# First attention: projections of 16 pieces placed in the attention's plan, row scores of the first heads beside them, low parts of the rotation on GpSimd

## What is computed

```python
x = x + 0.5 * _L0_ffn_ref(_layernorm(x), ...)
x = x + _L0_attn_ref(_layernorm(x), Wq, Wk, Wv, Wo)      # the changed part
x = x + 0.5 * _L0_ffn_ref(_layernorm(x), ...)

# _L0_attn_ref: B, S, H = 2, 1024, 256; 16 heads of 16
q, k, v = proj(Wq), proj(Wk), proj(Wv)
q, k = _apply_rope(q, cos, sin), _apply_rope(k, cos, sin)
scores = einsum('bhqd,bhkd->bhqk', q, k) / sqrt(hd) + causal
probs  = softmax(scores)
out    = einsum('bhqk,bhkd->bhqd', probs, v) @ Wo.T
```

## Time and profile before

| | us |
|---|---|
| median of 3 timed runs | 2742.62 (2741.81 to 2753.49) |
| profiled execution, whole | 2735.0 |
| its span | 2733.2 |
| PE busy in the span | 2529.4 (93%) |
| DVE busy | 1847.8 (68%) |
| ACT busy | 1396.2 (51%) |
| POOL busy | 369.8 (14%) |
| second tail of phase 0 ends on PE | 145.1 |
| first projection piece starts | 160.8 |
| last projection piece and values end | 226.3 |
| first T step starts | 275.55 |

### The profile page before, as it was taken

The page is one execution under the profiler, slowest core; times in us unless marked ns, Lnnn a source line. Parts: engine busy times, 40 slices in busy tenths (PEclk is TensorE's granted clock), DMA queues, the critical chain, the costliest instruction groups (busy, mean ns, idle before and its releaser), DMA issues. The chain is left out here.

```text
span 2733.2 us, 49842 instructions
## 1 busy us (share of the span) xinstructions
PE 2529.4 (93%) x16744; PEld 2111.5 (77%) x16744; DVE 1847.8 (68%) x4018; ACT 1396.2 (51%) x2464; POOL 369.8 (14%) x279
## 2 busy tenths in 40 slices
PE   3975898869899999998999999999999999999999
PEld 3963445358788888887877877878877788888888
DVE  4566767456567777776766766767767677777773
ACT  3430555645455555554655655555555555555553
POOL 1000000010121222221110010001100222122220
PEclk9996989879999999999999999999999999999999
DMA  4026133000000000000000000000000000000000
GB/s 157 0 78 146 25 48 48 2 32 4 27 31 22 10 31 31 0 20 20 1 20 1 19 19 0 19 19 0 19 0 32 32 32 1 32 31 0 31 0 31
DMA packets 18930, 73.28 MB, mean 27 GB/s; under 512 B 3328, under 2 KB 8192, under 8 KB 15616
## 3 DMA queue, kind: packets, MB, share of 16 engines
q1 hardware_dynamic: 18816, 71.78, 9.2%
HBM read 61.02 MB, written 10.49 MB: 26 GB/s over the span
## 5 line engine op out<-in xcount | busy, mean ns | idle before, releaser
L349 PEld LDWEIGHTS ps<-w,hid 128*128 128x128 f32 x5376 | 698.9, 190 | 56.5 <-DVE rb L425 14.6
L349 PE MATMUL ps<-w,hid 128*128 128x256 f32 x5376 | 719.5, 284 | 2.5 <-DVE rb L425 1.5
L318 PE MATMUL ps<-xT,w 128*128 (+1 forms) x2688 | 703.9, 398 | 0.1
L502 DVE TENSOR_TENSOR hid<-gel,hid 128x512 fp32r<-128x512 f32 x448 | 403.4, 911 | 360.8 <-ACT hid L392 352.4
L386 ACT ACTIVATE gel<-ps,b 128x512 f32<-128x512 f32 x448 | 306.9, 686 | 557.3 <-issue 543.6
L318 PEld LDWEIGHTS ps<-xT,w 128*128 128x128 f32 x2688 | 479.6, 190 | 79.5 <-issue 0.3
L392 ACT ACTIVATE hid<-gel 128x512 fp32r<-128x512 f32 x448 | 272.9, 622 | 0.0
L864 PE MATMUL ps<-pT,v_sb 128*128 128x512 f32 (+3 forms) x1152 | 261.6, 358 | 1.9 <-DVE pT L982 1.9
L838 PE MATMUL ps<-k_sb,q_sb 128*128 128x512 f32 (+3 forms) x1152 | 252.7, 353 | 3.0 <-DVE q_sb L999 3.0
L971 DVE TENSOR_REDUCE negmax<-ps 128x1 f32<-128x128 f32 (+7 forms) x256 | 192.3, 752 | 76.8 <-PE ps L841 75.5
L1431 DVE TENSOR_REDUCE nmx<-ps 128x1 f32<-128x512 f32 (+3 forms) x384 | 196.2, 553 | 70.1 <-PE ps L1302 53.5
(11 more groups left out here) (118 smaller groups left out, 2884.1 us busy)
## 6 DMA issues: line engine op xcount, KB each, us to landing
wraw<-in_wffn SPq DMA_DIRECT2D x12, 2048.0 KB, 7.7
wraw<-in_w_a SPq DMA_DIRECT2D x8, 1280.0 KB, 5.4
qk_dram<-rope_hl SPq DMA_DIRECT2D x16, 512.0 KB, 3.0
xT<-qk_dram SPq DMA_DIRECT2D x60, 128.0 KB, 8.3
qk_own<-qk_dram SPq DMA_DIRECT2D x36, 128.0 KB, 6.4
xb<-in_wffn SPq DMA_DIRECT2D x2, 2048.0 KB, 13.0
x<-in_x SPq DMA_DIRECT2D x4, 512.0 KB, 5.5
rot<-in_rot SPq DMA_DIRECT2D x1, 2048.0 KB, 18.7
```

Source lines behind the costliest of these rows:

```text
L318: last = nc.tensor.matmul(ps[:, HPS + j % 4, :], w[par][:, wp, 0, k * HIDDEN + j * PART:k * HIDDEN + (j + 1) * PART], xT[:, xp, k, bass.ds ...
L349: last = nc.tensor.matmul(y_ps[:, t, :], hid[:, hp, j % 4, t * PART:(t + 1) * PART], w[par][:, wp, 1, j * DIM:(j + 1) * DIM], start=j == 0 ...
L502: nc.vector.tensor_tensor(hid[:, 1, j % 4, :], gel[:, j % 4, :], hid[:, 0, j % 4, :].bitcast(f32), ALU.subtract).then_inc(low_done, 1)
```

## The change

1. The 16 projection pieces become items P of the plan. Their order is such that the first four (chunks 0 and 1, half 0, query and key) carry everything that groups 0 and 1 of heads need, the next four the other half of chunks 0 and 1, and the last eight chunks 2 and 3.
2. The tail of phase 0 (items S, L, G: the last second matmuls and take, the pieces of the norm, the transposes with the affine and the low input) is placed among the first four pieces, which need only chunks 0 and 1.
3. The splits of the attention's weights move into the first chunk of phase 0 (steps 4 to 7 of its eight).
4. Values are made two tiles at a time (12 matmuls of 256 columns, one copy of 512 elements), after pieces 4 to 11, in the PSUM bank of A.
5. From piece 6 on, three pairs U of row scores follow each piece: 30 of the 32 pairs of the lead stand among the pieces.
6. DVE keeps multiplies and sums; POOL makes the low parts of all 16 pieces, and its memsets stand among them (ones of the first buffers and of `v_f` after low part 1, of the second after low part 9, of the third after low part 15).
7. SP issues `load_heads(0)` after the store of piece 4, `load_heads(1)` after that of piece 9, and `load_heads(2)` after the feed-forward weights as before.
8. Buffers are laid out anew (`qk_own` becomes `q_own` and `k_own`, the third slot of `pT0` becomes `pT0_last`), so that the weights lie where phase 0 does not read.

```diff
+        PIECES = [(chunk, qk, half) for chunks, halves in (((0, 1), (0,)), ((0, 1), (1,)), ((2, 3), (0, 1)))
+                  for chunk in chunks for half in halves for qk in range(2)]
+        V_FROM, U_FROM, U_EACH = 4, 6, 3
...
+        def pool_rope_a0(pool):
+            def low_part(n):
+                pool.wait_ge(rope_high, n + 1)
+                nc.gpsimd.tensor_tensor(rope_hl[:, 1, n % 2, :], rope[:, 2, n % 2, :],
+                                        rope_hl[:, 0, n % 2, :].bitcast(f32), ALU.subtract).then_inc(rope_low, 1)
...
+            for n in range(N_PIECES):
+                low_part(n)
+                if n == 1:
+                    ones(QK[0])
+                    nc.gpsimd.memset(v_f[:], 1.0).then_inc(v_ones, 1)
+                if n == 2:
+                    nc.gpsimd.memset(nmx[:], 0.0).then_inc(v_ones, 1)
+                if n == 9:
+                    pool.wait_ge(proj_ready, 8)
+                    pool.wait_ge(v_ready, QT // 2)
+                    ones(QK[1])
+            pool.wait_ge(proj_ready, N_PIECES)
+            pool.wait_ge(v_ready, TILES // 2)
+            ones(QK[2])
...
+            for n in range(N_PIECES):
+                token, seq, qk, half, slot = rope_piece(n)
                 sp.wait_ge(rope_low, n + 1)
                 sp.dma_start(qk_dram[qk, half * PART:(half + 1) * PART, :, bass.ds(token, CHUNK)],
                              rope_hl[:, :, slot, :].bitcast(f32)).then_inc(rope_stored[slot], 16)
-                if n == N_PIECES // 2:
+                if n == 4:
...
                     sp.wait_ge(k_ones, 1)
                     load_heads(0)
+                if n == 9:
+                    sp.wait_ge(k_ones, 2)
+                    load_heads(1)
             sp.wait_ge(a_low, 4)
             load(1, 0, xb_raw)
             sp.wait_ge(k_ones, 3)
-            for g in (1, 2):
-                load_heads(g)
+            load_heads(2)
...
+            todo.append(("S",))
+            norm = {0: (0,), 1: (1,), 2: (2, 3), 3: (4, 5)}
+            for n in range(N_PIECES):
+                todo.append(("P", n))
+                todo += [("L", k) for k in norm.get(n, ())]
+                if n == V_FROM - 1:
+                    todo.append(("G",))
+                if n >= U_FROM:
+                    for j in range((n - U_FROM) * U_EACH, min((n - U_FROM + 1) * U_EACH, T_GROUP + AHEAD)):
+                        rows_of(j)
```

More of the change, by code:

```diff
@@ L1155, in pool_ones_a0, with rope_piece @@
[L1155 to L1164 removed]
+        def rope_piece(n):
+            chunk, qk, half = PIECES[n]
+            return chunk * CHUNK, chunk * CHUNK % SEQ, qk, half, n % 2
@@ new lines, in value_pair, with act_split_a0, dve_split_a0 @@
+        def value_pair(n):
+            return n - V_FROM if 0 <= n - V_FROM < TILES // 2 else None
+        def act_split_a0(act, piece):
+            act.wait_ge(a_loaded, 16)
+            tile, to, of = a0_split(piece)
+            nc.scalar.activation(tile[:, 0, to], xb_flat[:, of], ACT.Copy).then_inc(a_high, 1)
+        def dve_split_a0(dve, piece):
+            tile, to, of = a0_split(piece)
+            dve.wait_ge(a_high, piece + 1)
+            nc.vector.tensor_tensor(tile[:, 1, to], xb_flat[:, of], tile[:, 0, to].bitcast(f32), ALU.subtract)\
+                .then_inc(a_low, 1)
@@ L1303, in causal, with second_tail, piece, values @@
                                         steps_b[rows64, 4 * PART:4 * PART + HROW], start=False, stop=part == 1)
+            def second_tail():
+                for j in range(HT - 3, HT):
+                    pe_second(pe, tail(phase(0)), j)
+            def piece(n):
+                token, seq, qk, half, slot = rope_piece(n)
+                pe.wait_ge(a_low, qk + 2)
+                pe.wait_ge(xT_ready, S_ATT[0] - (2 if n < 8 else 0))
+                if n >= 2:
+                    pe.wait_ge(rope_taken, n - 1)
+                for swap in range(2):
+                    first = True
+                    for wp, xp in PARTS:
+                        for k in range(KD):
+                            at = ((2 * qk + swap) * KD + k) * DIM + half * PART
+                            last = nc.tensor.matmul(ps[:, 2 * slot + swap, :], w_qkv[:, wp, at:at + PART],
+                                                    xT[:, xp, k, bass.ds(token, CHUNK)], start=first,
+                                                    stop=(wp, xp) == (0, 0) and k == KD - 1)
+                            first = False
+                last.then_inc(proj_ready, 1)
+                if value_pair(n) is not None:
+                    values(value_pair(n))
+            def values(m):
+                if m == 0:
+                    pe.wait_ge(aff_done, S_ATT[0])
+                wait(pe, v_taken, m)
+                first = True
+                for t in range(2):
+                    for wp, xp in PARTS:
+                        for k in range(KD):
+                            tok = slice((2 * m + t) * PART, (2 * m + t + 1) * PART)
+                            last = nc.tensor.matmul(ps[:, AV0_PS, t * DIM:(t + 1) * DIM], xT[:, xp, k, tok],
+                                                    w_qkv[:, wp, V_W + k * DIM:V_W + (k + 1) * DIM], start=first,
+                                                    stop=(wp, xp) == (0, 0) and k == KD - 1, skip_group_check=True)
+                            first = False
+                last.then_inc(v_ready, 1)
             def rows(g, u, p):
                 qt, kc, width, diagonal = row_step(u)
+                if (g, u, p) == (0, 0, 0):
+                    pe.wait_ge(aff_done, S_ATT[0])
                 if (u, p) == (0, 0):
@@ L1388, in output @@
                 last.then_inc(ring_ready, 1)
-            run_a0(dict(U=rows, T=tiles, A=weighted, N=turn_maxima, C=turn_context, E=turn_back, O=output))
+            run_a0(dict(S=second_tail, P=piece, G=lambda: pe_transpose_chunk(pe, tail(phase(0))[1]),
+                        U=rows, T=tiles, A=weighted, N=turn_maxima, C=turn_context, E=turn_back, O=output))
         def act_attend_a0(act):
@@ L1615, in _ @@
                 walk(p, act, lambda at, prev: act_step(act, p, at, prev))
-                if k == 0:
-                    act_split_a0(act)
-                if p.last != "final" and k != 2:
+                if k == 1:
                     act_affine(act, tail(p)[1], CHUNKS - 1, 0)
```

204 lines of the change are left out of this document (81 added, 123 removed).

## The result

The changed kernel takes 2771.27 us, median of 12 runs (2765.85 to 2790.04); the kernel before beside it took 2742.22 (2731.61 to 2760.93). The ratio is 1.0108, 95% interval 1.0083 to 1.0134. The change costs 29 us between the medians.

The account below looks back on a forecast made before the run. PE's chain was taken as the bound: norm, heads' wait to 191.7, mixed stretch 81.6 and 24 to the first T gave 297.3 against 275.55, so 2742.6 + 21.8 = 2764.4 us, range 2741 to 2775.0.

Parts of the forecast that it names:

- Norm: Last chunk's norm beside the first four pieces: transposes start at 165, with 2.5 us allowed for POOL delaying the apply.
- The lock: VectorE operations with two SBUF inputs stand still for a GpSimd instruction; nothing counted outside the 2.5 us in the norm.
- the 3.48 of the earlier trace: Two DVE subtracts near 637 took 3.48 us instead of about 1.3, the first said to end only with a GpSimd instruction.
- POOL's low part: GpSimd's low part of 512 elements in each piece: 1.2 us, bounds 0.7 and 2.35.
- Heads of group 0: SP starts their 12 loads at about 176.3; first pair of scores at 191.7, PE idle 10 us ahead of it.
- Mixed stretch: PE's pieces 7 to 15, five double values and 27 pairs: 81.6 us, bounds 63 and 92.3; last piece done at 273.3.
- the usual 0.85: In the kernel before, each pair of row scores waits 0.85 us for the reductions of the pair before it.
- Last piece to first T: SP's last heads at +6.0, maxima issued +12.0 to +18.0, landing behind the heads: first T at +24, lower bound +20.
- Rival (4): SP's queue, not PE, sets the first T, so early rows are hidden anyway; no size or chance of its own.
- from the first T on the traces should run in parallel: After the first T step, the plan is unchanged, so the whole effect is the shift of that start, +21.8 us.
- rival 3: Low clock throughout the mixed stretch (92.3 us, +32 in all), or locks stretching the norm by 4 us; chance 0.10.
- Rival 1: Clock stays at 2.4 GHz in the mixed stretch: last piece at 254.7, first T at 279, +3; chance 0.22.

Follow-up runs that it names:

- low_on_dve: Changed kernel with the low parts back on VectorE right behind each sum, GpSimd keeping only its memsets; 2804.48 us, ratio 1.0231 to the kernel before.
- maxima_early: Changed kernel with SP issuing group 0's maxima between the stores of pieces 14 and 15, plus three satisfied ACT waits; 2744.65 us, ratio 0.9991 to the kernel before.
- before_more_waits: Kernel before with 114 satisfied waits added on ACT ahead of its T steps; 2745.27 us, ratio 1.0013 to the kernel before.

## Why the prediction was right, step by step

**Right.** The forecast was +21.8 by a first T step at 297.3; it came at 296.02, +20.5. The step "the plan from the first T step on is the same, so the change's effect is the shift of that start" held for the first attention (+20.9 at its end). Norm: transposes forecast at 165, were at 164.35. The apply lost 2.7 to POOL, 2.5 allowed. The lock that the prediction allows for, a VectorE instruction standing still for one of GpSimd, is in the traces as a length that ends with the GpSimd instruction: the four instructions of the stretched apply (1.38 before, 4.06 now) took 1.14, 1.34, 0.47 and 1.34 and each ended 0.15 behind one of POOL (161.38, 162.64, 163.04 and 164.30 against 161.23, 162.49, 162.89 and 164.15), and the two tiny instructions of low_on_dve took 1.65 and 3.87 beside memsets of 1.81 and 3.96. Of the 3.48 of the earlier trace rows the first subtract had its usual 0.69; it is the second, begun at 637.51, that took 2.88 and ended at 640.39, 0.55 behind POOL's. For the sums and multiplies of the rotation the prediction counted nothing, and they ran at 0.69 and 1.29 in the norm's stretch and in the mixed one.

**Right.** POOL's low part took 1.26 to 1.32 (forecast 1.2). Heads of group 0: issue from 175.75 (176.3), first pair at 191.14 (191.7), 10.30 idle (10).

**Mixed stretch, 78.7 instead of 81.6.** The nine pieces average 4.23 (I took 4.1), but they don't go up and down evenly: pieces 8 to 11 take 3.07, the first behind the stop and the last four 4.6 to 5.5. Pairs cost less than 1.3 where the values cover DVE, and more where they don't: behind pieces 12 to 15 the second pair waited 2.3 to 2.4 each time for multiplies, sum and reductions, where I had the usual 0.85 and about 0.85 more.

**Last piece to first T, 26.2 instead of 24.** SP began the last heads 6.0 and the maxima 12.0 behind the piece, both as forecast, and ended at +18.0; the mis-sized term is the landing, 8.2 after the last issue where I had 6. It nearly cancels against the mixed stretch (-2.9 and +2.2). Rival (4) of the prediction, that SP's queue and not PE sets the first T step, was put aside as "what the sum has"; maxima_early shows it is the very lever: with a last piece only 2.0 earlier the first T step is at 274.69.

**Missed.** The sentence "from the first T on the traces should run in parallel" failed in the second attention: +16 of the profile's +37. Whether it is also why the median's +29 stands above +21.8 is not shown, as the medians with the loop at rest don't show it. The prediction had no term for where a loop comes to lie in an engine's program; that 2771.27 still lies under the upper end of 2775.0 is luck, as that end was made for rival 3, which did not come. Rival 1 did not come as a whole either, the clock in the mixed stretch being 0.80 on the mean, but it held for pieces 8 to 11 (1.00 from 205.09 to 233.95). The 23 us that GpSimd's low parts save were in the sum only through the piece's chain, never priced by themselves, and my expectation for low_on_dve shows that I had not seen them.

## What to carry to other kernels

Work moved earlier uncovers what it used to cover: 32 pairs of row scores had hidden what stands in SP's queue, and moving them ahead of the last piece laid 26 us of it bare; ask of each queue what stands between the last producer and the first consumer, and put small urgent loads ahead of large ones that are needed later. Fillers for a second engine went in cheapest here one at a time between long matmul groups (0.66 each), and dearest in rows of three where nothing else covered that engine (over 2 each). When a hardware loop far from the change runs at another speed, compare the instruction queues' packets of the two traces before looking for a cause in its code.

## What the runs showed of the hardware

- One instruction more on ACT ahead of a hardware loop (49868 in the trace instead of 49867) took 25 packets of 8.2 KB off an instruction queue and 4.1 to 4.35 us of standstill off each of five rounds of that loop: 16 us in all. In the kernel before, 57 instructions more ahead of the loop brought the 25 packets, but a standstill of 2.1 to 2.3. low_on_dve, with 16 instructions more on DVE ahead of DVE's loop, drew 30 more again; nothing was run to show why.
- The trace can name an engine as the releaser of an idle time in which packets of the instruction queue came (4.09 put down to PE, three packets between 1528 and 1534); in before_more_waits it says "issue" at the same copy.
- With a plan that is the same, the first attention's T phase took 279 to 325 us, with a mean granted clock in its first 160 us between 0.95 and 0.69. Comparisons of kernels by single runs there are worth little under 1%.
- In low_on_dve two VectorE tensor-scalars on four elements a row, each 0.17 long in the changed kernel, took 1.65 beside GpSimd's memset of 2048 elements a row (1.81) and 3.87 beside that of 4608 (3.96), and ended 0.02 and 0.03 behind them (158.20 and 162.11 against 158.18 and 162.08). Not every instruction was held up: beside the same memset of 4608 in the changed kernel (157.30 to 161.23) a sum of 512 elements took its usual 0.69 at 159.05.
- In the kernel before, the matmuls of 512 columns of a piece started 0.427 apart at a granted clock of 0.50 (160.80 to 162.6), which is 1.20 columns a nanosecond, and 0.232 apart at 1.00 (165.71 to 168.7), which is 2.2. The 1.2 GHz of the text before is the first of these with one column taken for one cycle, and its 2.4 GHz is twice that: an estimate, as no trace gives the clock in GHz.
- The granted clock rose inside the two pieces of the kernel before that came from a wait: 0.50 from 160.80 to 163, 0.83 on the mean from 163 to 165.2 and 1.00 after; 0.50 from 220.2 to 224 and 0.71 from 224 to 226. With the pairs running it was 0.79 on the mean from 228 to 229 and 0.50 from 229 to 232. A pair's two matmuls of 512 columns took 0.79 there later, at 0.50 (252.58), and 0.49 in the changed kernel at 1.00 (211.48).
